# Two-layer transformer block on one core: some VectorE pieces moved behind the first two maxima of the next slot

## The chip, the cores and the metric

One Trainium2 chip, one of its cores. The metric is the device time of one execution in microseconds (us). Shown are the median of several executions and, beside it, one profiled execution with its own time and its trace. Engines are named TensorE (PE), VectorE (DVE), ScalarE (ACT), GpSimd (POOL) and SyncE (SP).

## The reference

Four sequences (1024 x 128, float32) go through two layers. Each layer normalises x, and adds an attention with 16 heads of width 8 and a feed-forward part to x.

- Layer 0: rotary attention without a mask, and a mixture of 8 experts with two chosen per token (128 to 512 to 128).
- Layer 1: causal attention, and a gated feed-forward part whose operands are rounded to blockwise FP4:

```python
gate = fp4_linear(x, w_gate)
y = fp4_linear(x, w_up)
h = jax.nn.silu(gate) * y
return fp4_linear(h, w_down)
```

## The kernel before, in words

The work is cut into eight phases, one for each layer and sequence, and laid out in advance as a list of 491 slots (class `Plan`). The list is the order of work of every engine: each engine's program walks over the slots and issues what the slot holds for it. Nothing else sets the order; engines meet only in semaphores.

A full slot holds, of attention, one **step** and one **quad**. A step is four score tiles (keys x queries, 128 x 512) of which ScalarE takes the exponential (L854) and that TensorE multiplies with the values in the next slot (tile `pO`). A quad is four score tiles (queries x keys) of a later phase, of which VectorE takes the row maxima: a plain reduction (L1201), or in layer 1, where the mask cuts the tile, a custom operation with a second instruction that reads the accumulator out (L1205). Maxima of the tiles 0 and 1 come first on VectorE, then the small steps of the slot, maxima of the tiles 2 and 3, the combination of maxima, and then the slot's other pieces (the list `xs`).

Each slot may also hold up to three **pieces** in `xs`: a piece is one more PSUM tile that TensorE fills after the step and the quad, and that ScalarE or VectorE reads. VectorE's own are named in `ON_VECTOR`. Those that matter here:

- `gu` with a last element 0, the **gate piece**: 352 columns. ScalarE takes a tanh of the tile (L939), VectorE then forms (tanh + 1) x gate from the same tile into `hs` (L1493). It waits for the tanh.
- `gu` with a last element 1, the **up piece**: VectorE multiplies `hs` with the tile (L1489). Behind it the quantisation of `hs` starts in small steps (`hq`, L1414 to L1426), and GpSimd rounds.
- `pj` with an empty last element, a **second-layer projection**: ScalarE copies the tile to bf16 (its high part, L548), VectorE waits for that copy and writes the tile minus the copy to `rb` (L1462), and in the next slot ScalarE copies that to bf16 (the `mid` part), between its exponentials 0, 1 and 2, 3.

All score tiles and pieces share one **ring** of seven PSUM banks, in the order in which TensorE issues them. In a full slot that is, with E for a step's tile and M for a quad's:

```
E0 M0 E1 M1 | values of the slot before | E2 M2 E3 M3 | pieces
```

TensorE waits before each tile until the tile seven places earlier has been read (function `vacant`). With one piece X in a slot, X has the bank that E3 of the next slot needs; with two pieces, the first has that of the next M2 and the second that of the next E3. A piece in the next slot reuses the bank of that slot's M0 when there is one of it.

There are 32 gate pieces, 32 up pieces and 16 second-layer projections. In 25 cases the gate piece is in one slot and its up piece in the next one, in 5 cases both are in one slot; one pair lies further apart, and the last one lies in slots that have no quad.

ScalarE's program in a slot: exponentials 0, 1; copy of `pO` if a group is done; the `mid` (and `hi`) copies; exponentials 2, 3; its share of the pieces (tanh and high-part copy among them).

Of the kernel before, what the change touches and what calls it, by code (L numbers as in the profile page):

```python
# [7 lines left out]
P = 128  # L8
HALF = 512
TH = HALF // P  # L10
DK = 8
G = 4
# [325 lines left out]
def two_layer_block(nc, x, wqa0, wqb0, wka0, wkb0, wv0, wo0, gate_w, gate_b, w1, b1, w2, b2wo,  # L338
# [26 lines left out]
    with ctx:  # L365
# [193 lines left out]
        def bank(e):  # L559
            return ring[plan.bank("X", plan.xs[e])]  # L560

        def filled(e):
            return plan.xs[e] + 1
# [9 lines left out]
        def sums(n):  # L573

            return hid[n % 2][:, :] if n in (2, 3) else ra[:, n % 2, :]

        def left(n):

            return oT[n % 2][:, :] if n in (2, 3) else rb[:, n % 2, :]
# [7 lines left out]
        with nc.Block() as block:  # L587
# [580 lines left out]
            def _(dve):  # L1168
# [4 lines left out]
                def own():  # L1173

                    if counted:
                        dve.wait_ge(s_dve, counted)
# [6 lines left out]
                def link(ins):  # L1183
                    count(ins)
                    own()

                def maxima(s, js):
                    if s["quad"] is None:
                        return
                    p, g, qt, kh = s["quad"]  # L1190
                    layer = PHASES[p][0]
                    for j in js:
                        k = 4 * plan.quads[s["quad"]] + j
                        w = HALF if layer == 0 else min(HALF, P * (qt + 1) - HALF * kh)

                        i = TH * (2 * (1 - j % 2) + j // 2) + qt % TH
                        dst = mparts[layer][:, qt // TH, i, kh:kh + 1]
                        src = ring[plan.bank("M", k)]
                        dve.wait_ge(s_m, k + 1)
                        if layer == 0 or P * (qt + 1) > HALF * (kh + 1):  # L1200
                            v.tensor_reduce(dst, src[:, 0:w], axis=X, op=ALU.max).then_inc(s_mr, 1)  # L1201
                        else:
                            if k >= 2:
                                dve.wait_ge(s_mr, k - 1)
                            v.tensor_tensor_reduce(out=junk[k % 2][:, 0:w], in0=src[:, 0:w],  # L1205
                                                   in1=diag[:, HALF - w:HALF], scale=1.0, scalar=NEG,
                                                   op0=ALU.add, op1=ALU.max, accum_out=dst).then_inc(s_mr, 1)
# [32 lines left out]
                def small_step(e):  # L1240
# [162 lines left out]
                    if kind in ("xq", "hq"):  # L1403
# [19 lines left out]
                        if k == 3:  # L1423
                            if kind == "xq":
                                dve.wait_ge(s_x, filled(("xT",) + w[1:]))
                            v.scalar_tensor_tensor(blocks(yq[:, 0:width]), blocks(src), 1.0 - 2.0 ** -22,  # L1426
                                                   wide(ri, width), ALU.mult, ALU.mult).then_inc(s_yq, 1)

                for s in plan.slots:
                    maxima(s, (0, 1))  # L1430
                    for e in s["small"][0] + s["small"][1]:
                        small_step(e)
                    maxima(s, (2, 3))
                    if s["combine"] is not None:
                        layer = PHASES[s["combine"][0]][0]
                        dve.wait_ge(s_mr, 4 * (plan.quads[s["quad"]] + 1))
                        link(v.tensor_reduce(mneg[:, :], mparts[layer][:, s["combine"][2], :, :], axis=X, op=ALU.max,
                                             negate=True))
                        link(v.tensor_copy(msplit[:, 0:G * TH], mneg[:, :]))
                        v.tensor_tensor(msplit[:, G * TH:2 * G * TH], mneg[:, :], msplit[:, 0:G * TH],  # L1440
                                        ALU.subtract).then_inc(s_ng, 1)
                    for e in s["small"][2]:
                        small_step(e)
                    for e in s["xs"]:
                        if plan.by[e][0] != "D":
                            continue
                        src = bank(e)
                        if e[0] != "gu" or e[3]:
                            dve.wait_ge(s_x, filled(e))
                        if e[0] == "pj":  # L1450
                            _, p, q, h, part = e
                            n = plan.parts[p, q, h]
                            half = slice(HALF * h, HALF * h + HALF)
                            if n >= 4:
                                dve.wait_ge(s_lo, n - 1)
                            if part == "a":
                                ins = v.tensor_tensor(sums(n), src[:, :], rc[:, half], ALU.mult)
                            elif part == "b":
                                ins = v.tensor_tensor(left(n), src[:, :], rs[:, half], ALU.mult)
                            else:  # L1460
                                dve.wait_ge(s_hi, n + 1)
                                ins = v.tensor_tensor(left(n), src[:, :], parts[:, q, 0, half], ALU.subtract)  # L1462
                        if e[0] == "lg":
                            ins = v.tensor_tensor(logit[:, :, :], src[:, 0:T * E].rearrange("p (t e) -> p t e", e=E),
                                                  gb[:, :].rearrange("p (o e) -> p o e", o=1).to_broadcast([P, T, E]),
                                                  ALU.add)
                        if e[0] == "rt":
                            ins = v.tensor_copy(before[:, :], src[:, 0:E * 2 * T + E])
                        if e[0] == "mtr":
                            k = plan.mtrs[e[1:]]  # L1470
                            if k:
                                dve.wait_ge(s_row, 64 * k)
                            ins = v.tensor_copy(mT[:, :], src[0:2 * G * TH, 0:P])
                        if e[0] == "fin":
                            _, p, g, qh = e
                            o4 = src[:, :].rearrange("p (q j w) -> p q j w", j=G, w=OW)
                            link(v.reciprocal(linv[:, :, :, :], o4[:, :, :, DK:2 * VC:VC]))
                            if g == 0 and (p or qh):

                                dve.wait_ge(s_x, filled(("of", p if qh else p - 1, 1 - qh)))  # L1480
                            for i in range(2):
                                dst = otok[:, :, G * DK * (2 * g + i):G * DK * (2 * g + i) + G * DK]
                                inv = linv[:, :, :, i].rearrange("p q (j o) -> p q j o", o=1).to_broadcast([P, TH, G, DK])
                                ins = v.tensor_tensor(dst.rearrange("p q (j w) -> p q j w", w=DK),
                                                      o4[:, :, :, VC * i:VC * i + DK], inv, ALU.mult)
                        if e[0] == "gu":
                            _, p, t, up = e
                            if up:
                                ins = v.scalar_tensor_tensor(hs[:, :], hs[:, :], 0.5, src[:, 0:F1], ALU.mult, ALU.mult)  # L1489
                            else:  # L1490
                                dve.wait_ge(s_th, T * PHASES[p][1] + t + 1)
                                dve.wait_ge(s_yq, plan.pools["hq", p, t])
                                ins = v.scalar_tensor_tensor(hs[:, :], th[:, :], 1.0, src[:, 0:F1], ALU.add, ALU.mult)  # L1493
                        if e[0] in ("down", "fp"):
                            _, p, i = e
                            b = PHASES[p][1]
                            own()
                            dst = xr[b % NX][:, i, :] if e[0] == "down" else flat(xr[b % NX], i)
                            if e[0] == "fp" and PHASES[p][0] == 0:
                                dve.wait_ge(s_xn, T * (p + 1))  # L1500
                            ins = v.tensor_tensor(dst, dst, src[:, 0:D] if e[0] == "down" else src[:, :], ALU.add)  # L1501
                        ins.then_inc(s_freed["D"], 1)
                        if e[0] in ("lg", "rt", "gu", "down", "fp") or (e[0] == "pj" and e[1] == 0 and e[4] == "b"):
                            dve.wait_ge(*freed(e))
                        if e[0] == "pj" and e[1] == 0 and e[4] == "b":
                            v.tensor_tensor(sums(n), sums(n), left(n), ALU.add).then_inc(s_sum, 1)
                    for e in s["small"][3]:
                        small_step(e)

# [49 lines left out]
```

## Time and profile before

| what | value |
|---|---|
| median of three executions | 1611.84 us (1610.04 to 1612.97) |
| the profiled execution, its own time | 1606.22 us |
| its span in the trace | 1604.5 us |
| TensorE busy | 1459.2 us (91%) |
| VectorE busy | 1338.2 us (83%) |
| ScalarE busy | 1129.7 us (70%) |
| GpSimd busy | 578.4 us (36%) |
| mean granted TensorE clock | 0.956 |

Busy times are the union of an engine's instructions. Neighbouring instructions of VectorE and ScalarE overlap at their ends in the records, so the mean length of one is more than its distance to the next. The ends of matmuls are modelled. "Idle before" is time in which the engine did nothing just before an instruction, with what ended it.

### The profile page before, as it was taken

The page shows a single profiled execution, that of the slowest core. Times are in us where ns is not written, and L with a number is a line of the kernel's source. Part 1 is how long each engine was busy: PE and PEld are TensorE (multiplying, and loading weights), DVE is VectorE, ACT ScalarE, POOL GpSimd, SP SyncE. Part 2 cuts the span into 40 slices and gives each one's busy share as a digit, 9 for nine tenths or more (in the row PEclk, how much of TensorE's full clock was granted, in tenths as well). Part 3 has the DMA queues.
Part 4 walks back from the last instruction along what each step waited for, and adds up shares of the span by engine and source line. Part 5 has one row for each costly group of instructions (what it writes and reads, how often), then busy time and mean ns, then how long its engine had stood idle before and what let it go on. Part 6 is the DMA issues. An engine that isn't in the chain of part 4 may idle for free.

```text
span 1604.5 us, 34217 instructions
## 1 busy us (share of the span) xinstructions
PE 1459.2 (91%) x10557; PEld 583.9 (36%) x10557; DVE 1338.2 (83%) x3450; ACT 1129.7 (70%) x2580; POOL 578.4 (36%) x531
## 2 busy tenths in 40 slices
PE   3978989999999899989999999989999988989986
PEld 1112344443333544432333444333433432323332
DVE  6999877789887698999888789889878779978991
ACT  2267678788787467777878767768878845765675
POOL 3002302103253456440242263660152464554443
PEclk8599999999999899999999999999999977989998
DMA  6403273333271452221451135123372100600000
GB/s 172 102 8 100 73 184 110 106 87 91 88 183 52 120 116 83 59 82 36 134 120 51 37 113 134 49 82 99 111 165 82 39 26 2 152 9 15 2 2 14
DMA packets 169833, 131.84 MB, mean 82 GB/s; under 512 B 31597, under 2 KB 143158, under 8 KB 169654
## 3 DMA queue, kind: packets, MB, share of 16 engines
q1 hardware_dynamic: 165562, 121.26, 28.5%
q0 software_dynamic: 4096, 8.40, 1.7%
q8 instruction: 91, 1.49, 0.4%
q14 instruction: 84, 0.69, 0.1%
HBM read 88.50 MB, written 40.50 MB: 80 GB/s over the span
## 4 chain that ended last, share of the span: by engine, by line
PE 58%; DVE 26%; issue 6%; ACT 5%; POOL 3%; DMA 1%; SPq 0%; another core or an unknown queue 0%; DVEq 0%; ACTq 0%; POOLq 0%
PE ring L542 38%; PE pO L542 17%; DVE mparts L1201 15%; PE ring L545 3%; ACT PR L854 3%; DVE junk L1205 2%; DVE xr L1381 1%; DVE stats L1251 1%; ACT hid L925 1%; DVE hs L1493 1%; DVE xr L1501 1%; DVE am L1414 1%; DMA b1r<-in_b 1%; ACT parts L548 0%; DVE hs L1489 0%
## 5 line engine op out<-in xcount | busy, mean ns | idle before, releaser
L854 ACT ACTIVATE PR<-ring 128x512 f32<-128x512 f32 (+3 forms) x1792 | 882.4, 557 | 344.8 <-PE ring L542 333.7
L1201 DVE TENSOR_REDUCE mparts<-ring 128x1 f32<-128x512 f32 x1280 | 808.5, 682 | 84.4 <-PE ring L542 77.1
L542 PE MATMUL ring<-QX,KX 50*128 50x512 bf16 (+3 forms) x1792 | 543.7, 366 | 77.2 <-DVE mparts L1201 35.5
L542 PE MATMUL ring<-KX,QX 48*128 48x512 bf16 (+3 forms) x1792 | 556.8, 374 | 14.2 <-DMA QX<-scratch 14.1
L542 PE MATMUL pO<-PR,VX 128*18 128x512 f32 (+3 forms) x3584 | 444.0, 568 | 6.5 <-ACT PR L854 5.2
L542 PEld LDWEIGHTS ring<-QX,KX 50*128 50x128 bf16 x1792 | 127.5, 94 | 609.0 <-ACT PR L854 220.3
L1205 DVE CUSTOM_DVE_ANT_0 junk<-ring,diag 128x384 bf16<-128x384 f32 (+3 forms) x512 | 228.8, 486 | 46.0 <-PE ring L542 41.2
L811 POOL TENSOR_SCALAR bq<-bq 128x352 f32<-128x352 f32 (+1 forms) x40 | 47.2, 1179 | 349.7 <-ACT bq L964 349.3
L784 POOL DMA_INDIRECT rows_in<-xn,at x64 | 63.7, 996 | 228.8 <-PE pO L542 144.8
L542 PEld LDWEIGHTS ring<-KX,QX 48*128 48x128 bf16 x1792 | 127.3, 94 | 33.6 <-DVE mparts L1201 17.9
L925 ACT ACTIVATE hid<-ring,b1r 128x128 f32<-128x128 f32 x368 | 105.0, 369 | 27.7 <-PE ring L542 26.2
L542 PE MATMUL ring<-yx,w1r 128*128 128x128 f32 x736 | 107.8, 291 | 7.7 <-DMA b1r<-in_b 4.8
L542 PEld LDWEIGHTS pO<-PR,VX 128*18 128x18 f32 x3584 | 60.6, 96 | 132.0 <-issue 88.0
L800 POOL DMA_INDIRECT ra<-rows_out,at x64 | 61.6, 963 | 125.4 <-PE pO L542 89.2
L542 PEld LDWEIGHTS ring<-yx,w1r 128*128 128x128 f32 x736 | 91.7, 196 | 34.3 <-DVE mparts L1201 23.3
L542 PE MATMUL ring<-w2r,hid 128*128 128x128 f32 x736 | 97.5, 275 | 0.0
L542 PEld LDWEIGHTS ring<-w2r,hid 128*128 128x128 f32 x736 | 93.2, 197 | 0.9 <-issue 0.5
L767 POOL TENSOR_TENSOR parts<-rb,parts 128x512 bf16<-128x512 f32 x30 | 35.0, 1166 | 115.3 <-ACT parts L548 115.3
L542 PE MATMUL ring<-identb,laterb 128*128 128x128 bf16 x512 | 75.2, 230 | 0.0
L825 POOL TENSOR_SCALAR yq<-yq 128x352 f32<-128x352 f32 (+1 forms) x40 | 60.3, 1508 | 3.3
L820 POOL TENSOR_TENSOR bq<-hq,bq 128x352 f32<-128x352 f32 x64 | 59.7, 933 | 4.6
L548 ACT ACTIVATE yx<-ring 128x256 f32<-128x256 f32 (+1 forms) x96 | 36.0, 375 | 35.2 <-PE ring L542 33.8
(165 smaller groups left out, 1349.8 us busy)
## 6 DMA issues: line engine op xcount, KB each, us to landing
w1r<-in_w SPq DMA_DIRECT2D x92, 256.0 KB
w2r<-in_w SPq DMA_DIRECT2D x92, 256.0 KB
scratch<-parts SPq DMA_DIRECT2D x48, 256.0 KB, 3.3
scratch<-parts SPq DMA_DIRECT2D x96, 128.0 KB, 2.3
KX<-scratch SPq DMA_DIRECT2D x64, 192.0 KB, 4.4
QX<-scratch SPq DMA_DIRECT2D x128, 96.0 KB, 5.0
xg<-rows_in SPq DMA_DIRECT2D x92, 64.0 KB
rows_out<-yx SPq DMA_DIRECT2D x92, 64.0 KB
```

The source lines that it names most:

```text
L542: return nc.tensor.matmul(dst, lhsT, rhs, start=start, stop=stop, **kw)
L545: return nc.tensor.transpose(dst, src, ident[0:src.shape[0], 0:src.shape[0]])
L548: return nc.scalar.activation(dst, src, ACT.Copy)
L784: nc.gpsimd.indirect_dma_start(xs[b % 2], bass.IndirectOffsetOnAxis(at[b % 2][:, c:c + 1], 0), xn[0][:, c % T, :], None).then_inc(s_sc[b], 16)
L800: nc.gpsimd.indirect_dma_start(yg[:, D * t:D * t + D], None, ys[b % 2], bass.IndirectOffsetOnAxis(at[b % 2][:, c:c + 1], 0)).then_inc(s_yg ...
L811: ins = nc.gpsimd.tensor_scalar(b_, b_, 1.0, None, ALU.max)
L820: ins = nc.gpsimd.tensor_tensor(b_, dst, b_, ALU.subtract)
L825: ins = nc.gpsimd.tensor_scalar(y, y, SHIFT, SHIFT, ALU.add, ALU.subtract)
L854: nc.scalar.activation(PR[:, n % 2, HALF * j + off:HALF * j + HALF], ring[plan.bank("E", k)][:, off:HALF], ACT.Exp, scale=SCALE).then_inc( ...
L925: ins = nc.scalar.activation(hid[N % 2][:, P * fc:P * fc + P], src[:, P * fc:P * fc + P], ACT.Relu, bias=b1r[N % 2][:, fc:fc + 1])
L1201: v.tensor_reduce(dst, src[:, 0:w], axis=X, op=ALU.max).then_inc(s_mr, 1)
L1205: v.tensor_tensor_reduce(out=junk[k % 2][:, 0:w], in0=src[:, 0:w], in1=diag[:, HALF - w:HALF], scale=1.0, scalar=NEG, op0=ALU.add, op1=ALU ...
```

## The change

VectorE's code for a piece becomes a function `piece(e)`, unchanged inside. The list of VectorE's pieces of a slot is cut at the first gate, up or second-layer projection: what stands ahead of it is issued where it was; the rest is kept and issued in the next slot, behind that slot's maxima 0 and 1 and ahead of its small steps. The small steps of group 3 thus come ahead of the moved pieces. The other engines' programs are the same.

```diff
+                def piece(e):
+                    src = bank(e)
...
+                left_over = []
                 for s in plan.slots:
                     maxima(s, (0, 1))
+                    for e in left_over:
+                        piece(e)
                     for e in s["small"][0] + s["small"][1]:
                         small_step(e)
                     maxima(s, (2, 3))
...
-                    for e in s["xs"]:
-                        if plan.by[e][0] != "D":
-                            continue
-                        src = bank(e)
...
+                    mine = [e for e in s["xs"] if plan.by[e][0] == "D"]
+                    late = [e[0] == "gu" or (e[0] == "pj" and e[4] == "") for e in mine]
+                    n_now = late.index(True) if True in late else len(mine)
+                    for e in mine[:n_now]:
+                        piece(e)
+                    left_over = mine[n_now:]
                     for e in s["small"][3]:
                         small_step(e)
```

By the plan 83 pieces are moved: the 64 gate and up pieces, the 16 second-layer projections, and three that stand behind one of them in their slot.

## Rows read from the trace of the kernel before

**Rows 1.** Instruction groups of VectorE by line and shape: busy us, mean ns, idle before.
```profile
L1201 DVE TENSOR_REDUCE mparts<-ring 128x1 f32<-128x512 f32 x1280 | 808.5, 682 | 84.4 <-PE ring L542 77.1 <-issue 1.1
...
L1493 DVE SCALAR_TENSOR_TENSOR hs<-th,ring 128x352 f32<-128x352 f32 x32 | 16.6, 520 | 22.9 <-ACT th L939 21.5 <-issue 1.3
L1489 DVE SCALAR_TENSOR_TENSOR hs<-hs,ring 128x352 f32<-128x352 f32 x32 | 16.6, 517 | 5.1 <-PE ring L542 4.7
...
L1462 DVE TENSOR_TENSOR rb<-ring,parts 128x512 f32<-128x512 f32 x16 | 11.1, 692 | 10.6 <-ACT parts L548 10.6
```
**Rows 2.** The chain that ended last, shares by engine (page, part 4).
```profile
PE 58%; DVE 26%; issue 6%; ACT 5%; POOL 3%; DMA 1%; SPq 0%; another core or an unknown queue 0%; DVEq 0%; ACTq 0%; POOLq 0%
```
**Rows 3.** Busy time by stretch: us, PE, PEld, DVE, ACT, POOL, PEclk, DMA share, GB/s.
```profile
430.00:1570.00 1140.00, 1065.34 (x7936) 433.70 (x7939) 966.67 (x2674) 825.60 (x1920) 491.97 (x437) 0.97 0.29 78
```
**Rows 4.** The same for one run of four second-layer projections.
```profile
768.00:786.00 18.00, 17.29 (x110) 6.07 (x109) 14.89 (x28) 16.08 (x35) 4.63 (x4) 1.00 0.41 125
```
**Rows 5.** Timeline 1041.3 to 1045.2, a gate piece and its up piece: start, length, what.
```profile
1041.58 0.60 PE L542 MATMUL ring<-KX,QX 48*128 48x512 bf16 x2
...
1042.20 0.52 DVE L1493 SCALAR_TENSOR_TENSOR hs<-th,ring 128x352 f32<-128x352 f32 x1 [0.21 <-ACT th L939]
1042.76 2.48 DVE L1201 TENSOR_REDUCE mparts<-ring 128x1 f32<-128x512 f32 x4
...
1043.33 0.38 PE L542 MATMUL ring<-QX,KX 50*128 50x512 bf16 x1
...
1043.64 0.86 PE L542 MATMUL ring<-wuT,xqT 128*128 128x352 f32 x2
...
1044.43 0.39 PE L542 MATMUL ring<-KX,QX 48*128 48x512 bf16 x1
...
1045.16 0.51 DVE L1489 SCALAR_TENSOR_TENSOR hs<-hs,ring 128x352 f32<-128x352 f32 x1
```
**Rows 6.** Timeline 890.3 to 896.5, another pair, with the shorter maxima of layer 1.
```profile
890.98 0.32 PE L542 MATMUL ring<-KX,QX 48*128 48x384 bf16 x1
...
891.49 0.52 DVE L1493 SCALAR_TENSOR_TENSOR hs<-th,ring 128x352 f32<-128x352 f32 x1 [0.72 <-ACT th L939]
892.40 0.38 PE L542 MATMUL ring<-QX,KX 50*128 50x512 bf16 x1
...
892.53 0.55 DVE L1205 CUSTOM_DVE_ANT_0 junk<-ring,diag 128x384 bf16<-128x384 f32 x1
...
893.01 0.55 DVE L1205 CUSTOM_DVE_ANT_0 junk<-ring,diag 128x384 bf16<-128x384 f32 x1
...
893.51 0.60 PE L542 MATMUL ring<-KX,QX 48*128 48x512 bf16 x2
...
895.74 0.60 DVE L1268 TENSOR_SCALAR xn<-xr,mv,rstd 128x128 f32<-128x128 f32 x2
```
**Rows 7.** Timeline 1217.9 to 1221.6, an up piece ahead of maxima whose tiles come late.
```profile
1218.32 0.60 PE L542 MATMUL ring<-KX,QX 48*128 48x512 bf16 x2
...
1218.42 0.52 DVE L1489 SCALAR_TENSOR_TENSOR hs<-hs,ring 128x352 f32<-128x352 f32 x1 [0.21 <-PE ring L542]
...
1220.18 0.51 DVE L1414 TENSOR_REDUCE am<-hs 128x22 f32<-128x352 f32 x1
```
**Rows 8.** Timeline 768.2 to 774.9, a second-layer projection and the slot behind it.
```profile
769.72 0.60 PE L542 MATMUL ring<-KX,QX 48*128 48x512 bf16 x2
...
770.71 0.69 DVE L1462 TENSOR_TENSOR rb<-ring,parts 128x512 f32<-128x512 f32 x1 [1.74 <-ACT parts L548]
...
771.44 0.64 ACT L548 ACTIVATE parts<-rb 128x512 bf16<-128x512 f32 x1
...
771.47 0.38 PE L542 MATMUL ring<-QX,KX 50*128 50x512 bf16 x1
...
772.06 0.33 PE L545 MATMUL ring<-ident,xg 128*128 128x128 f32 x1 [0.21 <-DVE mparts L1201]
...
774.18 0.60 ACT L548 ACTIVATE parts<-ring 128x512 bf16<-128x512 f32 x1 [0.48 <-PE ring L542]
```

More of the change, by code:

```diff
@@ L1427, in small_step @@
                                                    wide(ri, width), ALU.mult, ALU.mult).then_inc(s_yq, 1)
+                def piece(e):
+                    src = bank(e)
+                    if e[0] != "gu" or e[3]:
+                        dve.wait_ge(s_x, filled(e))
+                    if e[0] == "pj":
+                        _, p, q, h, part = e
+                        n = plan.parts[p, q, h]
+                        half = slice(HALF * h, HALF * h + HALF)
+                        if n >= 4:
+                            dve.wait_ge(s_lo, n - 1)
+                        if part == "a":
+                            ins = v.tensor_tensor(sums(n), src[:, :], rc[:, half], ALU.mult)
+                        elif part == "b":
+                            ins = v.tensor_tensor(left(n), src[:, :], rs[:, half], ALU.mult)
+                        else:
+                            dve.wait_ge(s_hi, n + 1)
+                            ins = v.tensor_tensor(left(n), src[:, :], parts[:, q, 0, half], ALU.subtract)
+                    if e[0] == "lg":
+                        ins = v.tensor_tensor(logit[:, :, :], src[:, 0:T * E].rearrange("p (t e) -> p t e", e=E),
+                                              gb[:, :].rearrange("p (o e) -> p o e", o=1).to_broadcast([P, T, E]),
+                                              ALU.add)
+                    if e[0] == "rt":
+                        ins = v.tensor_copy(before[:, :], src[:, 0:E * 2 * T + E])
+                    if e[0] == "mtr":
+                        k = plan.mtrs[e[1:]]
+                        if k:
+                            dve.wait_ge(s_row, 64 * k)
+                        ins = v.tensor_copy(mT[:, :], src[0:2 * G * TH, 0:P])
+                    if e[0] == "fin":
+                        _, p, g, qh = e
+                        o4 = src[:, :].rearrange("p (q j w) -> p q j w", j=G, w=OW)
+                        link(v.reciprocal(linv[:, :, :, :], o4[:, :, :, DK:2 * VC:VC]))
+                        if g == 0 and (p or qh):
+                            dve.wait_ge(s_x, filled(("of", p if qh else p - 1, 1 - qh)))
+                        for i in range(2):
+                            dst = otok[:, :, G * DK * (2 * g + i):G * DK * (2 * g + i) + G * DK]
+                            inv = linv[:, :, :, i].rearrange("p q (j o) -> p q j o", o=1).to_broadcast([P, TH, G, DK])
+                            ins = v.tensor_tensor(dst.rearrange("p q (j w) -> p q j w", w=DK),
+                                                  o4[:, :, :, VC * i:VC * i + DK], inv, ALU.mult)
+                    if e[0] == "gu":
+                        _, p, t, up = e
+                        if up:
+                            ins = v.scalar_tensor_tensor(hs[:, :], hs[:, :], 0.5, src[:, 0:F1], ALU.mult, ALU.mult)
+                        else:
+                            dve.wait_ge(s_th, T * PHASES[p][1] + t + 1)
+                            dve.wait_ge(s_yq, plan.pools["hq", p, t])
+                            ins = v.scalar_tensor_tensor(hs[:, :], th[:, :], 1.0, src[:, 0:F1], ALU.add, ALU.mult)
+                    if e[0] in ("down", "fp"):
+                        _, p, i = e
+                        b = PHASES[p][1]
+                        own()
+                        dst = xr[b % NX][:, i, :] if e[0] == "down" else flat(xr[b % NX], i)
+                        if e[0] == "fp" and PHASES[p][0] == 0:
+                            dve.wait_ge(s_xn, T * (p + 1))
+                        ins = v.tensor_tensor(dst, dst, src[:, 0:D] if e[0] == "down" else src[:, :], ALU.add)
+                    ins.then_inc(s_freed["D"], 1)
+                    if e[0] in ("lg", "rt", "gu", "down", "fp") or (e[0] == "pj" and e[1] == 0 and e[4] == "b"):
+                        dve.wait_ge(*freed(e))
+                    if e[0] == "pj" and e[1] == 0 and e[4] == "b":
+                        v.tensor_tensor(sums(n), sums(n), left(n), ALU.add).then_inc(s_sum, 1)
@@ L1443, in _ @@
                         small_step(e)
-                    for e in s["xs"]:
-                        if plan.by[e][0] != "D":
-                            continue
-                        src = bank(e)
[L1448 to L1506, printed above, removed]
```

## The prediction

> **What bounds the kernel now.** I read the stretches first, then VectorE's groups, then the timeline around single pieces. Between 430 and 1570 us, where nearly all moved pieces lie, TensorE shows work for 1065 of 1140 us, VectorE for 967 (85%) and ScalarE for 826 (72%) [rows 3]. The chain of waits is mostly TensorE's (58%) and VectorE's (26%) [rows 2]. TensorE's share is not pure work: it also has to wait for banks of the ring that VectorE has yet to free [rows 8]. So the loop is a ring of seven banks passed between three engines, VectorE the fullest of those whose busy time is work. A slot's shortest time on VectorE is its four maxima: they start 0.60 us apart ((2.48 - 0.68) / 3) [rows 1, 5].
>
> In that ring the moved pieces stand at a seam: VectorE idles 22.9 us before gate pieces (21.5 of it for the tanh), 5.1 before up pieces, 10.6 before the projections [rows 1]. That is 38.6 us, the most that could be closed; the last pair lies in slots without maxima and keeps what it waits.
>
> **The change, part by part.** No instruction is added or taken away. All that moves is VectorE's order: two maxima pass in front of a piece. The bank of the piece is then read later, and TensorE needs that bank for the last score tile of the very next slot.
>
> *A gate piece and its up piece in the next slot (25 of 32), first example* [rows 5]. M0 of the next slot is written at 1041.58 + 0.39 = 1041.97. VectorE now waits until 1042.20, and its maximum of tile 2 can start at 1042.76 + 1.20 = 1043.96. After the change: maxima at about 1042.03 and 1042.63, gate piece at 1043.23, maximum 2 at 1043.79 (a gate piece costs 0.56 start to start). VectorE gains 0.17 us. But E3 of that slot, which TensorE issued at 1043.33, now waits for the gate's bank until about 1043.80, 0.47 us later. Behind E3 stands the up tile: now 1043.64, then 1044.03, for E3 comes 0.23 before it. The up tile takes until the next score pair, 0.79 us. So M0 of the slot after, now written at 1044.82, is written at about 1045.20. VectorE has finished maximum 3 at 1044.99 and waits 0.2. Then maxima 0 and 1 (to 1046.40), the up piece (to 1046.95): maximum 2 at 1046.95. In the old order it is 1045.16 + 0.55 + 1.20 = 1046.91. Gain and loss cancel: +0.04 us. The hand-over from TensorE's modelled end to VectorE may add another 0.1 to 0.2.
>
> *Second example* [rows 6]. M0 is written at about 891.09 (the shown M1 at 890.98 + 0.32 = 891.30). Maxima at 891.14 and 891.62, gate piece at 892.10, maximum 2 at 892.66 instead of 893.01: gain 0.35. E3 goes from 892.40 to 892.70, so the next M0, written at 893.51 + 0.39 = 893.90, at 894.20. VectorE is done with maximum 3 at 893.62 and idles 0.58. Maxima 0 and 1 follow, of 0.62 each (in the old order they fill 894.51, which is 893.01 + 0.96 + 0.54 for the up piece, to 895.74), then the up piece, to 895.98, where the small step in the old order starts at 895.74. Loss: 0.25 us. In the old order the up piece filled just this time.
>
> *Up pieces whose maxima are late anyway* [rows 7]. M0 is written at 1218.71, and the up piece started at 1218.42 and was hidden. After the change: maxima at 1218.75 and 1219.35, up piece to 1220.47; its follower L1414, now at 1220.18, is 0.29 us later. About half of the ups are of this kind.
>
> I take 0.2 us per pair, between 0.04 and 0.29 and nearest to the second and third example: 25 x 0.2 = **+5.0 us**. Bounds: if the next M0 is never late, each pair gains the 0.17 to 0.35, in the middle 25 x 0.25 = -6 us; if the hold of E3 goes through whole, 25 x 0.47 = +12 us.
>
> *Five gate and up pieces in one slot.* Two banks are held, of the next M2 and E3; VectorE closes the wait. No row shows the new order; between a gain of 0.2 and a loss of 0.3 each. I take -0.1: **-0.5 us**.
>
> *Sixteen projections* [rows 4, 8]. ScalarE is the fuller engine there: 16.08 of 18 us, VectorE 14.89. VectorE waited 1.74 us for the high-part copy. After the change: M0 is written at 770.11, maxima at 770.15 and 770.75, the projection at 771.35, done by about 772.0. ScalarE's `mid` copy, at 771.44, waits for it to 772.0: 0.55 later, in front of two exponentials. TensorE's E3, at 771.47, also goes to 772.0; the tile behind it, which had waited for M0's maximum until 772.06, to about 772.25; and the next high-part copy, at 774.18 and fed by TensorE, goes back about 0.2. In slots with no other piece, and where the wait was short, the hold is longer (up to the 0.55). I take 0.3: 16 x 0.3 = **+4.8 us**. Bounds: if VectorE's start counts, which gains about 0.3, -5 us; if the 0.55 goes through whole, +9 us.
>
> *What moves with them.* `mtr`, `down` and others ahead of the cut stay. The small steps of group 3 pass one piece and gain a fraction of a us that nobody waits for. Of the three extra pieces one makes ScalarE's next high-part copy later; under 1 us together, taken as nothing. No DMA is issued by VectorE; SP's and GpSimd's orders are as before. GpSimd's rounding is fed by the small steps behind the up piece and idles most of the time; its wait shifts with VectorE.
>
> **The sum.** 5.0 - 0.5 + 4.8 = +9.3 us. Of VectorE's time in the stretch 15% is idle [rows 3], so some of this lateness falls into waits that end elsewhere; I keep 0.8 of it, **+7.4 us**. The profiled execution took 1606.2 us, so its like would take 1613.6; the median of the runs shown is 5.6 us above that execution, which gives 1619.2 us for the median.
>
> **Rivals.**
>
> 1. *The closed gaps win.* VectorE is the fullest real worker, and its wait for the tanh goes. If TensorE and ScalarE have enough slack to take the late E3, the slots come out at the gain of maximum 2. For it: ScalarE idles 28% of the stretch [rows 3], so late exponentials can be made up; against it: the two examples in which the next M0 comes late. It gives the low bounds, -6 - 1 - 5 = -12, at 0.8 about -10 us: 1602 us. It decides where the tile behind E3 is short. The Trainium skill (Perfetto Trace Analysis, "Identifying the Most-Contended Engine" and "Optimization Strategy") says to take the engine with the highest occupancy, leaving TensorE's matmul time out, and to work on the gaps between its slices. That speaks for this rival; taken to its end it would close all 38.6 us, for 1573 us. The trace only bears out a part, since M0 was itself not written when most of the longer waits began [rows 6, 7, 8].
>
> 2. *It is hidden anyway.* The gain on VectorE and the hold of the bank cancel, as in the first example, all over: within 3 us of 1612.
>
> 3. *Held banks stop ScalarE and TensorE in full.* +12 and +9 us and no absorption: 1633 us. It is the upper end of my forecast rather than another mechanism.
>
> That the change doesn't do what it says is not likely: each moved piece has maxima of the next slot to go behind, but for the last pair.
>
> **How the numbers follow.** Forecast (slower, held banks) 0.52, rival 1 0.27, rival 2 0.21. A measurement of this kernel can tell about 0.2%, 3.2 us, from no change. Slower by more 0.52, same 0.21, faster 0.27. The range goes from rival 1's value to the upper bound: 1601 to 1632 us; the forecast's own range is 1615 to 1632.
>
> **What would show it.** Right: VectorE's wait before L1493 falls from 22.9 us to under 6, and before L1462 from 10.6 to under 2; but the waits before L1201 and L1205 for TensorE's tiles grow by more than that, TensorE's weight loads of score tiles wait for `hs` and `rb` (they hardly do now), and ScalarE's copies of `rb` start to wait for L1462. VectorE's busy time stays at 1338 us. Wrong: if the waits before the maxima do not grow, M0 has slack that I did not see, and the kernel is faster; if they grow but the time does not, the pace is set elsewhere.

## The result, and the profile after

| | before | changed |
|---|---|---|
| median, executions of one comparison | 1611.32 us (4) | 1638.7 us (4; 1634.04 to 1645.15) |
| profiled execution, its own time | 1606.22 us | 1641.71 us |
| its span | 1604.5 us | 1640.0 us |
| granted TensorE clock, mean | 0.956 | 0.947 |

The changed kernel is slower: ratio 1.0185, 95% interval 1.0145 to 1.0225, about 27 us by the medians. In a second comparison it was 1638.61 against 1604.29 us, ratio 1.0201 (1.0171 to 1.023). The direction is the forecast's; the size is nearly four times the forecast's 7.4 us and outside the range. The two profiled executions lie 35.5 us apart, more than the medians, so sums read from their traces below are to be held against 35.5 and not against 27.

The page's first part, of the changed kernel (busy us, share of the span, instructions):

```profile
PE 1474.1 (90%) x10557; PEld 587.7 (36%) x10557; DVE 1342.9 (82%) x3450; ACT 1133.5 (69%) x2580; POOL 578.4 (35%) x531
```

No engine has more to do: VectorE's busy time went from 1338.2 to 1342.9 us. TensorE shows 14.9 us more for the same 10557 matmuls, at a granted clock of 0.947 for 0.956; the rest of the 35.5 us is time in which it waits. VectorE's groups by line and shape of the changed kernel (busy us, mean ns, idle before), to be held against [rows 1]; L1472 is the up piece, L1476 the gate piece, L1445 the projection, which were L1489, L1493 and L1462:

```profile
L1201 DVE TENSOR_REDUCE mparts<-ring 128x1 f32<-128x512 f32 x1280 | 811.9, 684 | 123.2 <-PE ring L542 113.9 <-issue 3.2
...
L1472 DVE SCALAR_TENSOR_TENSOR hs<-hs,ring 128x352 f32<-128x352 f32 x32 | 16.5, 515 | 1.4 <-PE ring L542 1.2
...
L1476 DVE SCALAR_TENSOR_TENSOR hs<-th,ring 128x352 f32<-128x352 f32 x32 | 16.4, 514 | 3.5 <-ACT th L939 3.5
```

The wait for the tanh is gone but for the last pair's 3.5 us (22.9 before), the wait before the ups fell from 5.1 to 1.4, and that before the projections, 10.6, no longer shows. In their place the wait before L1201 rose from 84.4 to 123.2 us, ended by TensorE; the four shapes of L1205 together have 74.4 us of it, 46.0 before. That is 34 us closed and 67 us opened. Who made TensorE late stands in the list of waits of the changed kernel (who waited for whom: us in total, times, longest):

```profile
PEld ring L542 <- DVE hs L1472: 16.9, 23, 1.7
PEld ring L542 <- DVE hs L1476: 14.5, 19, 1.6
...
PEld ring L542 <- DVE rb L1445: 13.0, 16, 1.4
ACT parts L548 <- DVE rb L1445: 11.6, 16, 1.3
```

Before, the same rows were 2.8, 3.0, 1.1 and 0.8 us. The pair of [rows 5] again, same slot, in the changed kernel (start, length, what, idle before):

```profile
1065.83 0.60 PE L542 MATMUL ring<-KX,QX 48*128 48x512 bf16 x2
...
1067.49 0.51 DVE L1476 SCALAR_TENSOR_TENSOR hs<-th,ring 128x352 f32<-128x352 f32 x1
...
1068.04 1.29 DVE L1201 TENSOR_REDUCE mparts<-ring 128x1 f32<-128x512 f32 x2
1068.06 0.09 PEld L542 LDWEIGHTS ring<-QX,KX 50*128 50x128 bf16 x1 [0.61 <-DVE hs L1476]
...
1068.06 0.39 PE L542 MATMUL ring<-QX,KX 50*128 50x512 bf16 x1 [0.32 <-DVE hs L1476]
...
1068.38 0.86 PE L542 MATMUL ring<-wuT,xqT 128*128 128x352 f32 x2
...
1069.17 0.39 PE L542 MATMUL ring<-QX,KX 50*128 50x512 bf16 x1
...
1069.63 1.29 DVE L1201 TENSOR_REDUCE mparts<-ring 128x1 f32<-128x512 f32 x2 [0.30 <-PE ring L542]
```

Count from the slot's first score tile, at 1041.58 before and 1065.83 here. E3 started 1.75 us after it and now 2.23; the up tile 2.06 and now 2.55; the next slot's first score tile 2.85 and now 3.34. E3's delay, 0.48 us, arrives in the next slot whole. VectorE's maximum of M2 came 2.38 after (1043.96) and now 2.21: it gains the 0.17 us of the prediction, and then idles 0.30 for the next M0.

All slots, worked out from the starts of TensorE's score matmuls in both profiled executions (E0 to E0 of the next slot, in us; "E3" is its start after E0, median):

| slot behind | slots | E3 before | E3 changed | slots longer by, in all | mean |
|---|---|---|---|---|---|
| a lone gate piece | 25 | 1.65 | 2.23 | 9.1 | 0.36 |
| a lone up piece | 26 | 1.90 | 2.23 | 11.0 | 0.42 |
| a projection | 14 | 1.75 | 2.40 | 6.5 | 0.46 |
| gate and up piece of one slot | 5 | 1.72 | 2.55 | 4.3 | 0.86 |
| gate or up piece and projection | 2 | | | 1.6 | 0.80 |
| the rest | 387 | 1.88 | 1.88 | 4.4 | 0.01 |

(E3 is over the slots that hold both a step and a quad; the last gate piece's slot holds no quad and is with the rest.) The loss sits in the 72 slots behind moved pieces. Of those slots 67 ran at a granted clock of 1.00 from start to end in both traces, and these alone grew by 26.9 us: a lower clock is not what made them longer. One place stands out, and has an experiment of its own below: three slots from 545 us on became longer by 2.28, 3.84 and 1.81 us. The first of them is among the 26, the other two are the rest's 4.4 us and more.

### The profile page after: what moved, and what is told of

Same layout as the page of the kernel before. It is cut to its first block and busy times, and to the rows that moved or that the text cites. A ratio compares the mean times of both kernels' runs of the same rounds, so it can differ in the third digit from the quotient of the medians.

```text
span 1640.0 us, 34223 instructions
## 1 busy us (share of the span) xinstructions
PE 1474.1 (90%) x10557; PEld 587.7 (36%) x10557; DVE 1342.9 (82%) x3450; ACT 1133.5 (69%) x2580; POOL 578.4 (35%) x531
## 5 line engine op out<-in xcount | busy, mean ns | idle before, releaser
L1201 DVE TENSOR_REDUCE mparts<-ring 128x1 f32<-128x512 f32 x1280 | 811.9, 684 | 123.2 <-PE ring L542 113.9
L542 PE MATMUL ring<-QX,KX 50*128 50x512 bf16 (+3 forms) x1792 | 552.6, 369 | 102.9 <-DVE mparts L1201 31.0
L542 PE MATMUL ring<-KX,QX 48*128 48x512 bf16 (+3 forms) x1792 | 565.3, 377 | 13.8 <-DMA QX<-scratch 13.8
L1205 DVE CUSTOM_DVE_ANT_0 junk<-ring,diag 128x384 bf16<-128x384 f32 (+3 forms) x512 | 231.3, 487 | 74.4 <-PE ring L542 66.7
L925 ACT ACTIVATE hid<-ring,b1r 128x128 f32<-128x128 f32 x368 | 105.0, 369 | 30.8 <-PE ring L542 29.6
L548 ACT ACTIVATE yx<-ring 128x256 f32<-128x256 f32 (+1 forms) x96 | 36.0, 375 | 36.9 <-PE ring L542 35.5
```

The lines of the kernel that those rows point to most:

```text
L542: return nc.tensor.matmul(dst, lhsT, rhs, start=start, stop=stop, **kw)
L548: return nc.scalar.activation(dst, src, ACT.Copy)
L925: ins = nc.scalar.activation(hid[N % 2][:, P * fc:P * fc + P], src[:, P * fc:P * fc + P], ACT.Relu, bias=b1r[N % 2][:, fc:fc + 1])
```

## The experiments

Theory H: the moved piece gives its bank back late; TensorE, which issues in order, stands in front of E3, and all that follows in the ring comes as much later. Theory V, the rival: TensorE has slack, and what costs is that a piece, an up piece above all, no longer fills a wait of VectorE. Theory C: much of the loss is the granted clock. All kernels but the hold are edits of the changed one; the edits are to VectorE's program. Ratios are to the kernel before, with 95% intervals; a cost taken from the ratio and one taken from the two medians can lie 3 us apart, so the text says which it is.

**One kind of piece at a time, and one maximum for two** (a first chip; before 1597.31 us, median of 21). Projections alone:

```diff
-                    late = [e[0] == "gu" or (e[0] == "pj" and e[4] == "") for e in mine]
+                    late = [e[0] == "pj" and e[4] == "" for e in mine]
```

> Only the 16 second-layer projections are moved behind two maxima; gate and up pieces stay. Held bank (theory H: the piece's bank is read later, TensorE stands in front of E3 of the next slot and everything behind it comes later by the same time): the slots behind a projection grew by 0.46 us each in the changed kernel, 16 x 0.46 = +7 us against before. Exposed VectorE work (theory V: what costs is that an up piece no longer fills a wait of VectorE, TensorE has slack): a projection has a wait in front of it, not behind it, so 0 or up to 5 us faster. Clock (theory C: half of the 27 us is a lower granted TensorE clock): +3 us with the clock back at 0.956.

Gate pieces alone, and up pieces alone:

```diff
+                    late = [e[0] == "gu" and not e[3] for e in mine]
```

> Only gate pieces (and an up piece of the same slot) are moved; up pieces of the next slot and projections stay. H: 26 slots behind a lone gate piece by 0.36 to 0.49 us and 5 slots with both by 0.86: about 9 + 4 = +13 us against before. V: the wait for the tanh is filled and nothing is exposed: 5 us faster. C: about +3 us and a clock of 0.956.

```diff
+                    late = [e[0] == "gu" and e[3] == 1 for e in mine]
```

> Only up pieces are moved, behind two maxima. H: the slots behind them grow by 0.42 us, 31 x 0.42 = +13 us. V: about half of the ups filled a wait, 15 x 0.55 = +8 us, and VectorE's idle time before the maxima behind them grows by as much. The two differ in the trace: by H TensorE's weight loads of a score tile wait for hs (L1472), and the slot is longer also where the next M0 was ready early.

All pieces, behind one maximum:

```diff
-                    maxima(s, (0, 1))
+                    maxima(s, (0,))
                     for e in left_over:
                         piece(e)
+                    maxima(s, (1,))
```

> All 83 pieces are moved, but behind one maximum instead of two. In the timeline at 1041 us the gate's bank is then free at about 1043.2, ahead of the 1043.33 at which TensorE issued E3 in the kernel before: no hold, and VectorE's wait for the tanh still filled. H: within 3 us of before, or up to 6 us faster. V: the up pieces are still behind a maximum that comes late, and half of the loss stays: +10 to +14 us. C: the clock goes back to 0.956 if TensorE is not held.

| moved | median us | ratio (interval) | clock |
|---|---|---|---|
| projections | 1608.88 | 1.0074 (1.0051 to 1.0096) | 0.952 |
| gates | 1602.87 | 1.0034 (1.0005 to 1.0062) | 0.958 |
| ups | 1628.69 | 1.0181 (1.0128 to 1.0234) | 0.941 |
| all, behind one maximum | 1607.80 | 1.0060 (1.0038 to 1.0082) | 0.950 |

The clock is the mean over the executions; the kernel before had 0.956. Every part alone is slower, gates and projections too, which V expected faster, since both have a wait in front that is now filled. The slots behind projections grew by 0.46 us, those behind gates by 0.40, as in the changed kernel. The sizes of H are less good. By the medians the projections cost 12 us where H said 7, and the gates 6 where it said 13: in the gates' trace the slots behind gate pieces have those 13 us, the slots behind ups give 2.9 back, and why no more than 6 is left isn't shown. The ups cost 31 us where H said 13 (slots behind them 0.65 us longer, 17 us in all), and one maximum for two brought the loss down only to 10 us where H said none: something was missing in H. Of C: among the 21 executions of the kernel before, time goes with the clock by 6.6 us for 0.01 (correlation -0.87), so the ups' clock accounts for some 10 of their 31 us, and gates lose at a clock that did not fall (0.958). The clock is a part, not the cause; the next two comparisons show it more sharply.

**The hold by itself, and controls** (a second chip; before 1604.29 us, median of 13).

> The changed kernel as it is, again, for a comparison on the chip of the three kernels beside it: 22 to 32 us over the kernel before, as measured the first time (27), although projections, gates and ups alone cost 12, 6 and 31 us, 48 in sum.

It came out at 34 us by the medians, 32 by the ratio.

The hold alone is an edit of the kernel before, in TensorE's program; `held` are the slots behind a moved piece:

```diff
                     for j in (2 * pair, 2 * pair + 1):
+                        if j == 3 and step is not None and quad is not None and id(s) in held:
+                            pe.wait_ge(s_mr, 4 * n_ + 2)
                         if step is not None:
                             vacant("E", 4 * n + j)
```

> The kernel before, with VectorE's order untouched, and one more wait on TensorE: in a slot behind a gate, up or second-layer projection, E3 waits until the maximum of M1 is taken. That is about when the moved piece gives its bank back in the changed kernel. No piece waits behind a maximum, so no piece is exposed. H (held bank): most of the loss is there again, +20 to +30 us, with the slots behind the pieces longer by 0.3 to 0.6 us each. V (exposed VectorE work): TensorE makes the hold up, within 5 us of before.

> Only up pieces are moved, behind one maximum. The bank is free 0.6 us earlier than behind two (VectorE's maxima start 0.60 us apart). H: of the 31 us that ups alone cost behind two maxima at most a fifth is left: 0 to +6 us. V: VectorE still waits for M0 with the up piece undone, and the piece comes 0.55 us on top: +8 us or more, half of the slots behind ups longer.

The small steps alone: `left_over` is taken out, and the pieces are issued in their own slot behind the small steps of group 3.

> Nothing is moved to the next slot; only the small steps of group 3 come ahead of the gate, up and projection pieces of their own slot, as they do in the changed kernel. All theories: no difference, within 3 us of before; if it is slower by 5 or more, the order of the small steps has a part in the loss.

| kernel | median us | ratio (interval) |
|---|---|---|
| the changed kernel again | 1638.61 | 1.0201 (1.0171 to 1.0230) |
| the hold alone | 1637.94 | 1.0196 (1.0165 to 1.0228) |
| ups behind one maximum | 1624.39 | 1.0105 (1.0064 to 1.0145) |
| small steps first | 1607.86 | 1.0003 (0.9975 to 1.0030) |

The hold alone, with VectorE's order untouched, costs what the change costs: 34 us by the medians, a little over H's 20 to 30, and far from V's 5. It does so at an almost unchanged clock: 0.953 in the mean of its executions against 0.954 before, and in its trace TensorE is busy 3.3 us more than before while the span is 30.8 us longer. So theory C can't account for it. The same slot in its timeline (L1500 is the gate piece, L1208 the maxima):

```profile
1059.59 0.60 PE L542 MATMUL ring<-KX,QX 48*128 48x512 bf16 x2
...
1060.21 0.52 DVE L1500 SCALAR_TENSOR_TENSOR hs<-th,ring 128x352 f32<-128x352 f32 x1 [0.21 <-ACT th L939]
1060.77 2.50 DVE L1208 TENSOR_REDUCE mparts<-ring 128x1 f32<-128x512 f32 x4
...
1062.12 0.39 PE L542 MATMUL ring<-QX,KX 50*128 50x512 bf16 x1 [0.61 <-DVE mparts L1208]
```

E3 starts 2.53 us after the slot's first tile, and the slots behind gates are 0.69 us longer in the mean, those behind projections 0.96: each wait is a little longer than the changed kernel's (E3 at 2.51 and 2.78 in the medians, against 2.23 and 2.40), because here the gate piece's own wait still lies in front of the maxima. Behind ups it is small (E3 at 2.01, slots 0.05 longer). So the equal totals are not a proof that the hold accounts for each microsecond of the change, above all not at the ups, nor of the changed kernel's loss through the piece described below; they do show that TensorE has no slack for such a hold, which was the forecast's hope and V's premise.

The order of the small steps has no part that shows: the interval reaches from 4 us faster to 5 us slower. The ups behind one maximum cost 17 us by the ratio, 20 by the medians. H had said 0 to 6 and V 8 or more, so this total speaks for V. The slots behind ups say otherwise: they grew by 0.19 us each, 5 us in all, only 7 of the 26 by more than 0.2, and 1.7 of the 5 us lie in one slot. That slot and the two behind it grew by 7.7 us together. This led to the stretch at 545 us.

**The piece that went back with its up piece.** In the slot at 540 us VectorE has three pieces: `fp`, an up piece, and the rotary product b of a later phase's projection (`pj`, L1459 before, L1442 after). The cut at the up piece takes the product along. The changed kernel's timeline there:

```profile
545.98 1.29 DVE L1201 TENSOR_REDUCE mparts<-ring 128x1 f32<-128x512 f32 x2 [3.12 <-PE ring L542]
...
547.19 0.51 DVE L1472 SCALAR_TENSOR_TENSOR hs<-hs,ring 128x352 f32<-128x352 f32 x1
547.73 0.69 DVE L1442 TENSOR_TENSOR rb<-ring,rs 128x512 f32<-128x512 f32 x1
547.85 0.37 PE L542 MATMUL ring<-QX,KX 50*128 50x512 bf16 x1 [0.67 <-DVE hs L1472]
...
548.50 1.26 POOL L759 TENSOR_TENSOR ra<-ra,rb 128x512 f32<-128x512 f32 x1 [8.99 <-DVE rb L1442]
...
549.86 0.63 ACT L548 ACTIVATE parts<-ra 128x512 bf16<-128x512 f32 x1 [2.17 <-POOL ra L759]
...
551.12 0.48 PE L542 MATMUL ring<-QX,KX 50*128 50x384 bf16 x1 [1.40 <-ACT PR L854]
```

VectorE idles 3.12 us before M0, which is late here, though the up piece's tile has long been written and the product's follows before M0's. It starts the product at 547.73, 2.48 us after the slot's first tile, where it was 0.16 after it before the change (543.17 and 543.01). Then GpSimd's sum waits for the product, ScalarE's high-part copy 2.17 us for the sum, in front of its exponentials 2 and 3, and TensorE 1.40 us for those. After that TensorE runs slower; the stretch from 540 to 570 us, before and changed (us, busy by engine, then PEclk):

```profile
540.00:570.00 30.00, 28.38 (x221) 14.55 (x221) 22.98 (x87) 17.18 (x48) 12.11 (x11) 0.92 0.53 118
```

```profile
540.00:570.00 30.00, 27.68 (x165) 15.16 (x163) 14.01 (x59) 10.54 (x30) 3.58 (x3) 0.66 0.25 69
```

The granted clock there is 0.66 for 0.92, and 165 matmuls are done for 221 (the changed kernel is 2 us behind at its start). In windows of 5 us from 540 on, it was 0.54 and then 1.00 throughout before the change, and 0.54, 0.78, 0.56, 0.50, 0.57 and 1.00 in the changed kernel: it was low already ahead of the stall, rose, and fell once more. The third comparison (on the second chip again; before 1605.95 us, median of 24) takes it apart. Such slots left whole (77 pieces are then still moved; the text below says 78, a miscount):

```diff
                     n_now = late.index(True) if True in late else len(mine)
+                    if not all(late[n_now:]):
+                        n_now = len(mine)
```

> The changed kernel, but the three slots in which another piece stands behind a gate or up piece keep all of it in place (83 moved pieces become 78). In one of them (the slot at 540 us) the rotary product b of a later phase went back with its up piece, and the three slots from there took 8 us more in the changed kernel, at a granted clock of 0.62. If that one piece costs what it shows: 24 to 28 us over before instead of 33. If that stretch is only a clock that falls here or there in any execution: no difference from the changed kernel, 31 to 35.

With that edit, behind one maximum:

> Behind one maximum, without the three slots. Held bank: E3 is issued 0.01 to 0.1 us later than before, the slots behind gates and projections are as long as before or 0.05 shorter, behind ups 0 to 0.1 longer: between 4 us faster and 4 us slower. If exposed VectorE work counts, +8 us as with the ups alone behind one maximum.

Only such slots moved (the same edit with `if all(...)`):

> Only the three slots with another piece behind a gate or up piece are moved, behind two maxima; the other 77 pieces stay. If the rotary product that goes back is what costs: +6 to +10 us, all of it from 543 to 560 us, with the granted clock of that stretch under 0.7. Otherwise within 3 us of before.

Gates and projections alone, behind one maximum, without such slots (by the way the cut is written the five slots with gate and up piece then stay in place as well):

> Gate pieces and projections behind one maximum, ups in place, without the three slots: only the pieces that have a wait in front of them. Held bank: nothing is held and the waits of 22.9 and 10.6 us are partly filled: 2 to 6 us faster than before. Otherwise: no difference.

| kernel | median us | ratio (interval) |
|---|---|---|
| two maxima, the three slots left whole | 1633.12 | 1.0160 (1.0119 to 1.0201) |
| one maximum, the three slots left whole | 1606.31 | 1.0002 (0.9979 to 1.0025) |
| only the three slots moved | 1612.46 | 1.0049 (1.0023 to 1.0074) |
| gates and projections, one maximum | 1602.51 | 0.9968 (0.9945 to 0.9991) |

Moving the three slots alone costs 8 us by the ratio (3.7 to 11.9; 6.5 by the medians), and in its trace the three slots behind the rotary product are longer by 2.29, 3.84 and 1.75 us, 7.9 in sum. Its stretch:

```profile
540.00:560.00 20.00, 17.67 (x89) 8.11 (x88) 8.04 (x26) 7.17 (x18) 3.58 (x3) 0.59 0.14 41
```

With those slots left whole, one maximum for two takes the loss from 27 us (by the medians) to none, at nearly the same mean clock (0.952 and 0.953). That is the sharpest test of H: in both kernels the same 77 pieces stand behind a maximum whose tile can be late, as V has it, and what differs is that the piece comes, and the bank is free, one maximum earlier. V said +8 us. The slots behind ups, which V is about, grew by 0.04 us in the mean, and half of them by nothing. The same slot once more, in that kernel:

```profile
1043.59 0.60 PE L542 MATMUL ring<-KX,QX 48*128 48x512 bf16 x2
...
1044.65 0.51 DVE L1476 SCALAR_TENSOR_TENSOR hs<-th,ring 128x352 f32<-128x352 f32 x1
...
1045.20 1.89 DVE L1201 TENSOR_REDUCE mparts<-ring 128x1 f32<-128x512 f32 x3
...
1045.34 0.38 PE L542 MATMUL ring<-QX,KX 50*128 50x512 bf16 x1
...
1046.44 0.39 PE L542 MATMUL ring<-QX,KX 50*128 50x512 bf16 x1
```

The gate piece is issued behind one maximum, its wait for the tanh is filled, and E3 starts 1.75 us and the next slot 2.85 us after the first tile, as before the change. In the medians E3 stands at 1.72 behind gates (1.65 before) and 1.80 behind projections (1.75). Leaving the ups in place, which had no wait worth filling, gives 1602.51 against 1605.95 us: 0.3% faster, with an interval that just leaves out 1. It is the best kernel of the study, by little, and as one of eleven kernels compared it may owe that to chance.

## Why the prediction was right in direction and wrong in size

- **The bound.** Right: a ring of banks between three engines. Wrong in what it made of the idle shares [rows 3]: 28% of ScalarE idle (rival 1) and 15% of VectorE (the factor of 0.8) were read as slack that takes up a late E3. TensorE issues in the order of the program and is the part without slack, and the others' idle time is mostly waiting for it (of ScalarE's 475 us idle before the change, 334 are waits of its exponentials for TensorE's tiles). The hold alone, 2%, shows it.
- **A gate piece and its up piece.** The single steps came out as worked: VectorE's gain 0.17 us (measured 0.17), E3 later by 0.47 (0.48), VectorE's new wait 0.2 (0.30). The up tile and the next slot's first tile came later by 0.49 where 0.39 was written. What failed is the step from there to 0.2 us per pair: it read the cost on VectorE, at its third maximum two slots on, where the lateness is hidden by old waits, and not on TensorE, where the next slot had already begun 0.39 later by its own arithmetic. And it counted one hold per pair: the up piece holds its bank as well. Measured 0.36 + 0.42 = 0.78 us per pair, 20 us for 5.0 (18 without the slot of the rotary product); the upper bound of 12 was for one hold.
- **Five slots with both pieces.** Sign wrong: -0.5 us, measured +4.3. Two banks, of M2 and E3, are held there; E3 starts 0.83 us later.
- **Projections.** Mechanism right, the wait of ScalarE's copy for L1462 above all, 0.8 us in sum before and 11.6 after. Mis-sized: 0.3 us taken, 0.46 measured, of a hold of 0.65; in sum 4.8 against 6.5, and 8.1 with the two mixed slots.
- **What moves with them.** Taken as nothing, under 1 us. One of the three extra pieces cost 7.9 us in two traces and 4.5 in two others. The prediction named who waits for it, and did not follow the chain through ScalarE's order to TensorE and the clock. After the 15 us missed at the pairs this is the largest miss.
- **The factor of 0.8** for lateness that falls into other waits had no ground. The 387 other slots gave nothing back.
- **Rival 1** (closed gaps win) described the gains and not the price; a part of it may be true once nothing is held: 3 us with one maximum, at the edge of what can be told. By the Trainium skill (Perfetto Trace Analysis, "Optimization Strategy") one finds the gaps between the slices of the engine that one works on, and makes what they wait for start sooner or end faster. This change filled them with other work instead: 34 us of VectorE's gaps were closed and the time rose, so a closed gap alone is no gain here. **Rival 2** (cancels) is false behind two maxima and true behind one. **Rival 3**, called the upper end of the forecast, came nearest. Not all of a hold goes through (in the slots, 0.36 us of 0.58 behind gates and 0.46 of 0.65 behind projections), but there are two per pair. With the second one its 21 us would have been 33, and the range would have held the result.
- **The signs named** were right: VectorE's waits before the pieces fell as said (3.5 us before the gates, nothing shown before the projections), those before the maxima grew by more, and weight loads wait for `hs` and `rb`.

What stays open: how much of the ups' cost is V's. Behind them the hold alone costs 0.05 us a slot while the changed kernel costs 0.42, with E3 later in it (2.23 against 2.01): in the hold kernel the up piece starts before M0 is written in 19 of 25 slots, and E3 then waits for two maxima; in the changed kernel it waits for two maxima and the piece. So the piece's lost place in VectorE's wait makes the hold longer. That it costs without a hold is not seen: behind one maximum, where it is lost as well, the slots behind ups grew by 0.04 us. Open, too, is why the ups alone cost more than the slots behind them show, beyond the stretch at 545 us and the clock.

## What to carry to other kernels

A wait of a reader in a ring of PSUM banks can be filled with other reads only as long as the bank that it delays is not the next one that the writer needs: count the places from the piece to the tile that reuses its bank, and see when the writer issues that tile. Here one maximum fitted in (0 to -0.3%) and two did not (+1.6%, without the rotary product). The cost of a hold is read where the in-order writer starts its next block, not on the engine whose wait was filled; and when a piece is moved with a cut in a list, look at each piece that goes along, for its own chain can be the dearer one.

## What was unexpected of the hardware

- TensorE's idle time of 1.40 us behind the late rotary product was followed by a granted clock of 0.56, 0.50 and 0.57 in the three windows of 5 us from 550 on, where it was 1.00 before the change. Of the 8 us that the three slots took more, 5.6 came in the two slots after the stall itself. The first slot behind the product took 3.58 us before and 5.86 to 5.87 in each of four traces that move it behind two maxima. The next one took 5.12 before, 8.96 in two of them and 7.33 or 7.34 in the two others. The changed kernel itself has one trace of each kind, so how long the lower clock lasts differs from execution to execution.
- Between executions of the kernel before on one chip, the time follows the mean granted clock (correlation -0.87 over 21): 1592.20 us at 0.961, 1604.47 us at 0.943.
- The same kernel's median differed between comparisons: 1611.32, 1597.31, 1604.29 and 1605.95 us, the last two on one chip. Costs of whole kernels are therefore taken within one comparison only; the traces are compared across them.
